# Three seams at once: statistics beside the interpolated weights, a first tile made in the recurrence, the last sequence of the third attention in another order

## Time and profile before

| | us |
|---|---|
| median of 3 runs (lowest, highest) | 2515.89 (2515.77, 2516.43) |
| the profiled execution | 2521.32 |
| its span, first to last instruction | 2519.6 |

### The profile page before, as it was taken

One profiled execution on the slowest core, in us unless ns is written; L12 is line 12 of the kernel. 1 busy time (PEld: TensorE's weight loads), 2 busy tenths in 40 slices (PEclk: granted clock), 3 DMA queues, 4 the chain that ended last, 5 costly groups with the idle time before them and its releaser, 6 DMA issues. The chain is left out here.

```text
span 2519.6 us, 30138 instructions
## 1 busy us (share of the span) xinstructions
PE 2371.6 (94%) x10329; PEld 1275.9 (51%) x10329; DVE 1360.5 (54%) x3458; ACT 773.2 (31%) x2046; POOL 729.0 (29%) x721
## 2 busy tenths in 40 slices
PE   8999999989999999999879999869998899998799
PEld 4455455555355655555555555534443344444454
DVE  5544343125111314776666777876764355555897
ACT  1134344203011114555531010311110356654333
POOL 3655455204000004321123333310000255656200
PEclk9999999989999998999959999989999899999799
DMA  7026200024375542110052222530000311211000
GB/s 191 1 79 230 73 17 8 1 69 123 107 263 198 205 135 80 53 42 18 1 179 101 92 88 100 220 124 6 5 9 13 109 50 54 59 37 34 27 13 14
DMA packets 93677, 203.30 MB, mean 81 GB/s; under 512 B 18580, under 2 KB 37428, under 8 KB 91864
## 3 DMA queue, kind: packets, MB, share of 16 engines
q1 hardware_dynamic: 87384, 188.26, 22.3%
q0 software_dynamic: 6144, 13.13, 1.9%
HBM read 150.45 MB, written 45.94 MB: 78 GB/s over the span
## 5 line engine op out<-in xcount | busy, mean ns | idle before, releaser
L3612 POOL TENSOR_SCALAR a_p<-a_p,a_li 100x257 f32<-100x257 f32 x252 | 188.3, 767 | 118.3 <-DVE a_li L3469 118.3
L671 POOL TENSOR_SCALAR a_shared<-a_shared,a_li 128x361 f32<-128x361 f32 x104 | 131.5, 1265 | 183.8 <-DVE a_li L579 183.8
L3215 PE MATMUL bank<-l_early,a_ctx 128*128 128x512 f32 (+1 forms) x384 | 180.2, 615 | 0.0
L2601 PE MATMUL bank<-f_xT,s_w 128*128 128x400 f32 x512 | 179.2, 504 | 0.6 <-ACT f_xT L2665 0.6
L2176 PE MATMUL bank<-s_wgu,f_xT 128*128 128x512 f32 x384 | 168.9, 593 | 0.7 <-ACTq L2383 0.7
L2601 PEld LDWEIGHTS bank<-f_xT,s_w 128*128 128x128 f32 x512 | 98.1, 192 | 77.0 <-issue 2.9
L1891 POOL DMA_INDIRECT a_got<-slots_y,slots_of x32 | 33.5, 1047 | 318.9 <-POOLq L1231 310.1
L2176 PEld LDWEIGHTS bank<-s_wgu,f_xT 128*128 128x128 f32 x384 | 72.7, 190 | 92.2 <-issue 90.5
L3215 PEld LDWEIGHTS bank<-l_early,a_ctx 128*128 128x128 f32 (+1 forms) x384 | 68.8, 188 | 85.0 <-issue 84.9
L351 PE MATMUL bank<-a_wk,a_ctx 128*128 128x512 f32 (+1 forms) x192 | 95.5, 617 | 9.4 <-DMA a_wk<-in_L_xattn_Wk 5.7
L729 ACT ACTIVATE a_shared<-a_shared,a_nm 128x361 f32<-128x361 f32 x104 | 62.1, 597 | 99.5 <-DVE a_nm L573 99.5
(11 more groups left out here) (452 smaller groups left out, 4898.0 us busy)
## 6 DMA issues: line engine op xcount, KB each, us to landing
slots_x<-zero SPq DMA_DIRECT2D x4, 4096.0 KB, 27.0
f_triple<-in_L_ffn_triples SPq DMA_DIRECT2D x16, 768.0 KB, 4.2
rounded<-f_triple SPq DMA_DIRECT2D x16, 768.0 KB, 3.3
s_whole<-in_L_ffn_w SPq DMA_DIRECT2D x24, 512.0 KB, 3.8
e_wg<-in_L_ffn_w_gate SPq DMA_DIRECT2D x16, 704.0 KB, 4.4
e_wu<-in_L_ffn_w_up SPq DMA_DIRECT2D x16, 704.0 KB, 6.5
e_wd<-in_L_ffn_w_down SPq DMA_DIRECT2D x16, 512.0 KB, 4.3
e_xg<-slots_x SPq DMA_DIRECT2D x16, 512.0 KB, 5.4
```

What stands on the lines that cost most here:

```text
L671: pool.tensor_scalar(p[s % NP], p[s % NP], li[:, b % 2, h:h + 1], None, ALU.mult).then_inc(normed, 1)
L2601: mm = nc.tensor.matmul(banks[f % 2][:, 0:GT], w[:, kc, f * P:(f + 1) * P], xT[:, kc, :], start=(kc == 0), stop=(kc == KC - 1))
L3215: mm = nc.tensor.matmul(bank[0:m, :], columns[:, kc], w[:, kc, :], start=(kc == 0), stop=(kc == KC - 1))
L3612: pool.tensor_scalar(p[g % 2][j][:, lo:hi], p[g % 2][j][:, lo:hi], li[:, h, i:i + 1], None, ALU.mult) \
```

## The change

Three parts change together.

**A, the last sequence of layer 3's attention.** For b = 7 every engine gets an order of its own. PE does the out-projection of sequence 6 right behind the scores of group 1, before any head is turned, and turns the first tile only at the very end. DVE rounds that tile behind the last `take_output`. ACT takes the sums of all 24 pieces. SP sends piece 20 behind the moves of the rows.

**B, layer 1's statistics.** `stage_stats` is gone. Statistics, roots, and the normalized, turned and copied rows of the first four sequences are made in the interpolation's block; the loads of triples and weights stand at the start of the next one. The summaries are copied by DVE, which adds the bias at once.

**C, the recurrence.** The bias is in the summaries now. ACT adds summary and shift, at places between its weight copies given by `ADD_AT`. DVE makes each shift ahead of time. The second block layer's 32-row tile is measured, rounded, turned and copied inside the recurrence and handed over as `lead`; SP moves sequence 7's rows behind triple 7 for this.

```diff
 # B: stage_L1_ffn, POOL, PE, ACT, DVE
                         pool.tensor_tensor(pts[t % 3][:], pts[t % 3][:], pw[t % 3][:], ALU.mult).then_inc(multiplied, 1)
+                        b = t - (PARTS_W - B)
+                        if b >= 0:
+                            pool.wait_ge(var_made, b + 1)
+                            pool.tensor_tensor(rstd[:, b:b + 1], var[:, b:b + 1], k.half[0:S, :], ALU.pow).then_inc(rstd_made, 1)
...
+                    for b in range(GB):
+                        pe.wait_ge(xn_made, b + 1)
+                        pe.wait_ge(laid, (PARTS_W - 1) * N + b + 1)
+                        for kc in range(KC):
+                            mm = nc.tensor.transpose(k.bank[b][:, kc * S:(kc + 1) * S], xn[b][:, kc * P:(kc + 1) * P],
+                                                     k.ident[0:S, 0:S])
+                        mm.then_inc(x_turned, 1)
...
                     for t in range(PARTS_W):
+                        if t == PARTS_W - 1:
+                            for b in range(GB):
+                                dve.wait_ge(rstd_made, b + 1)
+                                dve.tensor_scalar(xn[b][:], k.res[:, b, :], stat[:, b, 0:1], rstd[:, b:b + 1],
+                                                  ALU.subtract, ALU.mult).then_inc(xn_made, 1)
...
+                        b = t - 2
+                        if 0 <= b < B:
+                            step(dve.bn_stats(stats[:, b, :], k.res[:, b, :]))
+                            step(dve.bn_aggr(stat[:, b, :], stats[:, b, :]))
+                            dve.tensor_scalar(var[:, b:b + 1], stat[:, b, 1:2], LN_EPS, None, ALU.add).then_inc(var_made, 1)
 # B: stage_columns_ffn, ACT, then DVE
-                act.wait_ge(all_made, 1)
-                act.copy(early.all8[:], b_u[1][0:B, :]).then_inc(all_copied, 1)
...
+                    if n == FC - 1:
+                        dve.wait_ge(all_made, 1)
+                        dve.tensor_tensor(early.all8[:], b_u[1][0:B, :], early.bout[0:B, :], ALU.add).then_inc(all_copied, 1)
 # C: stage_L2_recurrence, ACT
+        ADD_AT = [0, 1, 4, 6, 8, 10, 13]
...
+                def add_shift(i):
+                    act.wait_ge(shift_made, i + 1)
+                    act.wait_ge(got, i + 1)
+                    if i >= 2:
+                        act.wait_ge(y_made, i - 1)
+                    act.activation(added[i % 2], g_bank[i % 4][0:S, :], ACT.Identity, bias=shift[:, i:i + 1]).then_inc(added_made, 1)
+
+                add_shift(0)
                 for t in range(FC):
...
+                    if t in ADD_AT:
+                        add_shift(ADD_AT.index(t) + 1)
 # C: DVE
+                def shifted(i):
+                    n = 2 * i
+                    dve.wait_ge(rstd_made, roots.index((i, 0)) + 1)
+                    dve.scalar_tensor_tensor(shift[:, i:i + 1], stat[:, n, 0:1], -1.0, rstd[:, n:n + 1], ALU.mult, ALU.mult) \
+                        .then_inc(shift_made, 1)
                 def second(i):
-                    dve.wait_ge(rstd_made, roots.index((i, 0)) + 1)
-                    step(dve.scalar_tensor_tensor(shift[:, i:i + 1], stat[:, n, 0:1], -1.0, rstd[:, n:n + 1], ALU.mult, ALU.mult))
-                    dve.wait_ge(got, i + 1)
-                    dve.scalar_tensor_tensor(added[:], g_bank[i % 4][0:S, :], shift[:, i:i + 1], bout[:], ALU.add, ALU.add)
+                    dve.wait_ge(added_made, i + 1)
...
                 first(0)
                 first(1)
+                shifted(0)
                 for i in range(B):
                     second(i)
+                    if i == 0:
+                        shifted(1)
                     if i + 2 < B:
                         first(i + 2)
                     if i >= 1:
                         third(i - 1)
+                    if i + 2 < B:
+                        shifted(i + 2)
+                    if i == B - 4:
+                        measure_last_tile()
+                    if i == B - 3:
+                        round_last_tile()
 # C: POOL, behind rb(6)
+                    if (i, which) == (B - 2, 0):
+                        pool.wait_ge(x_var_made, 1)
+                        pool.tensor_tensor(x_rstd[:], x_var[:], k.half[0:m_last, :], ALU.pow).then_inc(x_rstd_made, 1)
 # A: stage_L3_attention, PE's order for b = 7
+                scores(B - 1, 1)
+                project_out(B - 2)
+                scores(B - 1, 2)
+                turn_heads(B - 1, 0)
+                outputs(B - 1, 0)
+                scores(B - 1, 3)
+                for g in range(1, G):
+                    turn_heads(B - 1, g)
+                    outputs(B - 1, g)
                 project_out(B - 1)
...
+                turn_first_tile()
 # A: DVE's order for b = 7
+                all_maxima(B - 1, 1)
+                measure_first_tile()
+                inverses(B - 1, 1)
+                add_output(B - 2)
+                all_maxima(B - 1, 2)
+                copy_heads(B - 1, 0)
+                inverses(B - 1, 2)
+                all_maxima(B - 1, 3)
+                copy_heads(B - 1, 1)
+                inverses(B - 1, 3)
+                scale_last_heads()
+                copy_heads(B - 1, 2)
+                copy_heads(B - 1, 3)
+                take_output(B - 1)
+                round_first_tile()
                 add_output(B - 1)
 # A: ACT; done[6, 2] is piece 16, done[7, g] are 17, 18 and 19 to 23
+                    if n == B - 1:
                         signs(b, 2)
+                    exponentials(n, 0)
...
+                for g in range(1, G):
+                    exponentials(B - 1, g)
+                    signs(B - 1, g - 1)
                 take_first_tile()
```

More of the change, by code:

```diff
@@ L104, in _ @@
             sp.wait_ge(stored, 16)
[L107 to L140, removed]
 GH = 4
@@ L2522, with stage_columns_ffn @@
 HALF = TRIPLE // 2
-def stage_columns_ffn(k, tag, gate, up, down, raw, rounded, early, recurrence):
+def stage_columns_ffn(k, tag, gate, up, down, raw, rounded, early, recurrence, stat, rstd, xT):
     nc = k.nc
@@ L2561, in _ @@
             def _(sp):
+                for i in range(2):
+                    sp.dma_start(tri[i][:], raw[i]).then_inc(tri_in[i], 16)
+                early.load(sp, recurrence, early_in)
                 one = lambda a, t: a[t] if isinstance(t, int) else a[bass.ds(t, 1)].rearrange("a p n -> (a p) n")
@@ L3025, in _ @@
                         summary(t // 2 + 1)
+                pe.wait_ge(x_made, 1)
+                pe.wait_ge(copied, 3 * FC - 3)
+                for kc in range(KC):
+                    mm = nc.tensor.matmul(t_bank[0][:, kc * m_last:(kc + 1) * m_last], xn[:, kc * P:(kc + 1) * P],
+                                          k.ident[0:m_last, 0:m_last], is_transpose=True, start=(kc == 0), stop=(kc == KC - 1))
+                mm.then_inc(x_turned, 1)
 def stage_L2(k, early, third, weights):
@@ L3131, in stage_L3_attention @@
                               [("v", n, 1)] + [("kT", n, fb) for fb in range(KC)] + [("qT", n)], []][g]
-                if b > 0 and g == (3 if more else 0):
+                if b > 0 and more and g == 3:
                     order += [("o", b - 1)]
-                if not more and g == 2:
-                    order += [("x0",)]
-        order += [("o", B - 1)]
+        order += [("o", B - 1), ("x0",)]
         R = Ring(k, "a3_ring", [k.bank[4], k.bank[5], k.bank[7]], order)
@@ L3361, in _ @@
                     outputs(b, 2)
-                    if more:
-                        turn_keys(n)
-                        turn_queries(n)
-                        values(n, 2)
-                        scores(n, 0)
+                    turn_keys(n)
+                    turn_queries(n)
+                    values(n, 2)
+                    scores(n, 0)
                     turn_heads(b, 3)
-                    if more and b > 0:
+                    if b > 0:
                         project_out(b - 1)
@@ L3380, in _ @@
                 step = Link(dve, stepped)
-                def sum_pieces(first, n):
-                    for i in range(first, first + n):
-                        dve.wait_ge(piece_in[i % 4], (i // 4 + 1) * 16)
-                        dve.tensor_reduce(third.sums[:, i:i + 1], third.whole[i % 4][:], AX.X, ALU.add,
-                                          apply_absolute_value=True).then_inc(last_pieced, 1)
                 def measure(b):
```

236 lines of the change are left out of this document (108 added, 128 removed).

## The result

The changed kernel takes 2498.53 us (median of 4 runs, 2497.65 to 2501.48) against 2516.16 for the kernel before beside it (2515.77 to 2522.47): a ratio of 0.9929, 95% interval 0.9917 to 0.9942, 17.6 us less. The forecast was 2499.9. Run again in another session the changed kernel came to 2502.61 against 2520.08, a ratio of 0.9930 (0.9917 to 0.9944).

A forecast was written before the change was run, and what follows sets the result against it. TensorE is busy nearly all the time, so time can be won only at seams between stages; VectorE bounds the recurrence. Terms -10.0 + 4.8 - 10.8 = -16.0 take the median 2515.89 to 2499.9 us, range 2495 to 2506.

The forecast's parts named there:

- B, -10.0: End of interpolation: first statistics move into VectorE's gaps, first gate product 10.4 us earlier, less 0.4 for the clock.
- VectorE's end was put at +1.7: Interpolation: 10.4 us of added measurements, normalizations and waits against 8.7 of gaps make VectorE end 1.7 us late.
- Nothing else is later: Interpolation's end: TensorE's transposes and ScalarE's copies of x lie beside VectorE's last four copies, costing nothing more.
- The 0.4 for the clock: First gate products: a new gap of about 1.4 us may lengthen the half-clock time; 0.4 us taken, 0.7 possible.
- C, +4.8: Recurrence and second block layer's first tile: 13.2 us paid in VectorE's queue, 8.4 won at the next stage's start.
- +13.2: Recurrence: five VectorE stalls of 2.6 us behind GpSimd's queue plus the tile's work, less removed additions, lengthen it 13.2 us.
- The lock-out: Recurrence: VectorE and GpSimd excluding each other on SBUF would lengthen five stalls by 0.4 us, 2 us; not counted.
- A, -10.8: Last sequence of the third attention: reordering wins 11.9 us, less 1.1 for the clock; bounds -15 to -4.
- From here GpSimd paces: Third attention's last sequence: GpSimd's 14 heads of 1.44 us without a gap set the last out-projection's start, 2337.9.
- The 1.1 for the clock: Next block after the third attention: TensorE stands 2.8 us, its clock may fall, costing 0 or 2.2; 1.1 taken.
- No rival: Included: attention's tail gains half, 2505.7 (0.14); y waits for ScalarE in the recurrence, 2520.9 (0.05); change misdescribed (0.02).
- Rival 1: The recurrence doesn't stall because roots come in time: C is -8.7, all -29.5, 2486.4 us; chance 0.13.

The follow-up runs named there:

- Experiment 1: The changed kernel with GpSimd's addition of bias to residual moved one root later, both roots ahead of its wait: 2494.12 us, ratio 0.9886.
- experiment 9: The changed kernel with heads 2 and 3 of group 2 of the last attention sequence scaled by VectorE instead of GpSimd: 2503.30 us, timed once.
- experiment 7: The changed kernel with the four normalizations placed one ahead of each of the interpolation's last four parts, not all before the last: 2496.95 us, timed once.
- experiment 5: The kernel of Experiment 1 with ScalarE's additions of shift and summary one or two triples earlier, TensorE's summary products to match: 5305 us.
- experiment 6: The kernel of experiment 5 with the last sequence's two row moves on SyncE's queue issued in the next block: 2492.00 us, timed once.
- experiment 3: The changed kernel with part B undone, first statistics again in their own block behind the interpolation: 2513.87 us, ratio 0.9968.
- experiment 4: The changed kernel with part C undone, the earlier recurrence and the second block layer's first tile made in that layer: 2496.58 us, ratio 0.9900.
- the repetition of 5: The same kernel as experiment 5, run once more on another chip: 2477.32 us, timed once.

## Why the prediction was right

**B, -10.0; measured -9.9.** VectorE's end was put at +1.7 and came at +1.2, and at +0.4 to +0.6 in the eight other traces: measurements and gaps nearly cancel, as put. "Nothing else is later" was wrong: ScalarE's copies of x end 1.2 us after VectorE in all of them. The two misses have opposite signs. The first gate product came 9.7 earlier in the first trace and 10.25 to 10.48 in the eight, for 10.4: that the number is met so closely is luck. The 0.4 for the clock can't be told from the scatter: from the first gate product to the first silu 7.79 us pass before and 7.60 after, and 7.2 to 8.6 in the other runs, of which 8.44 is one without B. The triple landed at 1318.88, under the products, as put.

**C, +4.8; measured +4.3, and 3.4 to 4.6 with what follows.** The recurrence grew by 12.8 for +13.2 (45.40 to 58.21), by five stalls of the size and in the place that the order of GpSimd's queue gave (period 6.81 for "near 6.9"); the first product came 8.5 sooner behind VectorE's end (11.07 to 2.54) for 8.4. Experiment 1 shows the mechanism: with the order changed and nothing else, the stalls go. The lock-out was rightly left at nothing here: with VectorE standing still, both roots take 1.07.

**A, -10.8; measured -12.1.** The last out-projection starts 31.0 us after sequence 5's, where it took 44.9: 13.9 for the 14.4 of the sum, but for a wrong reason. "From here GpSimd paces" fell in experiment 9. Its 14 heads end at 2321.54, just as TensorE comes to them (2321.98), so that a sum along the wrong engine gave the right number, by luck. The serial work behind it was put at 10.6 with the out-projection and took 9.9. The 1.1 for the clock was the mis-sized term. TensorE did lose 1.31 us (8.38 for 7.07), but where the clock doesn't fall, it then waits for VectorE's rounding of the next tile and for its first hidden values (0.18 and 0.77 us in experiment 7), and the next 16 products start 8.67 us after the first in both; 159.2 us to the end pass with the fall and without it.

No rival came true. Rival 1, a recurrence that doesn't stall, is what experiments 1 and 5 make of the kernel: r of 47.6, where its sum of -8.7 asks for 47.8.

## What to carry to other kernels

A wait in a helper engine's queue holds everything queued behind it: before a consumer is moved forward, read the producer's queue from its last wait on, and put the short work that others need ahead of the long work that waits. A block ends with its slowest queue, the one that only issues transfers included. When an engine's busy time and the forecast end agree, take work off that engine once and see, before calling it the bound.

## What the hardware showed unexpectedly

VectorE's y (residual and `added` in SBUF) and GpSimd's addition exclude each other: the one that starts 0.05 to 0.09 us later takes 1.77 us instead of 0.74 or 1.26 (rows of experiment 6). The Trainium skill (SBUF — State Buffer, Who interferes with whom) has this lock held for the whole instruction; the trace agrees but for some 0.2 us: strictly one behind the other, the later one would take 1.91 and 1.96.

The clock between the groups of layer 1 (the section on the result) fell in eight of thirteen traces while TensorE was busy without a gap, on 8-column products and transposes; that cost 4.2 us.

TensorE stood for the same 2.75 us ahead of the third feed-forward in nine traces. In five it began the next 32 products at the half level (1.2 GHz), and they took 8.38 to 8.43 us; in four (experiments 3, 4, 7 and the repetition of 5) it stayed at 2.4 GHz:

```profile
2338.93 7.07 PE L2138 MATMUL bank<-s_w,l_early 128*128 128x512 f16 x32 [2.75 <-PEq L3126]
```

The Trainium skill (TensorE: Matmul & The Clock Gate, What's actually happening) has an engine that stood idle long enough fall back to the lower level; here the same idle time was followed by a fall in five of nine traces.

One execution (experiment 5) took 5305 us, with the granted clock recorded as 1.0 throughout and VectorE as busy as ever. Groups of the page, it and then the changed kernel:

```profile
L2138 PE MATMUL bank<-s_wgu,s_lead 128*128 128x512 f32 x192 | 182.0, 1147 | 0.0
```

```profile
L2138 PE MATMUL bank<-s_wgu,s_lead 128*128 128x512 f32 x192 | 84.4, 592 | 0.0
```

The groups of products that both pages list took 1.8 to 2.4 times as long; the same kernel took 2477.32 us on another chip. The recorded clock does not show it, and no run settles its cause.
